# Layer normalisation from batch-norm statistics, a tile at a time, in a fused convolution, attention and expert kernel

## The reference

```python
x = x + _L0_conv_ref(_gn(x), L0_conv_weight)            # x: 8 x 64 x 56 x 56
t = _to_tokens(x)                                        # 8 images x 3136 tokens x 64 channels
t = t + _L1_attn_ref(_ln_t(t), Wq, bq, Wk, bk, Wv, bv)   # one head of 64
t = t + _L1_ffn_ref(_ln_t(t), gate_w, gate_b, w1, w2, w3)  # 16 experts, the best 2 of each token
x = _from_tokens(t, x)

def _ln_t(v, eps=1e-05):
    m = jnp.mean(v, axis=-1, keepdims=True)
    s = jnp.var(v, axis=-1, keepdims=True)
    return (v - m) / jnp.sqrt(s + eps)
```

## Time and profile before

| what | value |
|---|---|
| median of 3 runs | 2724.68 us (2722.92 to 2728.44) |
| the profiled execution | 2721.7 us, of which the span is 2720.0 us |
| TensorE busy | 2506.6 us (92%) |
| VectorE busy | 1832.1 us (67%), 5227 instructions |
| ACT busy | 1317.0 us (48%) |
| GpSimd busy | 1016.9 us (37%) |
| mean granted TensorE clock | 0.964 |

### The profile page before, as it was taken

How to read it: one execution, slowest core, us unless ns; L and a number is a source line. 1 busy time by engine, 2 the same in 40 slices (tenths; PEclk the granted TensorE clock), 3 DMA queues, 4 the chain that set the end, 5 groups by cost and what they waited for, 6 DMA issues and landing times.

```text
span 2720.0 us, 46270 instructions
## 1 busy us (share of the span) xinstructions
PE 2506.6 (92%) x13821; PEld 1604.3 (59%) x13821; DVE 1832.1 (67%) x5227; ACT 1317.0 (48%) x2986; POOL 1016.9 (37%) x1097
## 2 busy tenths in 40 slices
PE   5899999999999999999999999999999999997773
PEld 3455555566666666566666666566665656554662
DVE  5577677767676777677766777676867776674432
ACT  2344444455555555455545555455555555453542
POOL 2022005300343425342444324442344324465665
PEclk8899999999999999999999999999999999997866
DMA  2033101111112122121212122222121111122432
GB/s 75 26 90 77 45 22 48 49 34 39 53 49 66 52 54 59 55 58 49 62 52 62 48 57 64 58 53 53 54 55 52 43 49 51 54 55 62 121 94 53
DMA packets 226556, 152.95 MB, mean 56 GB/s; under 512 B 100240, under 2 KB 216720, under 8 KB 226320
## 3 DMA queue, kind: packets, MB, share of 16 engines
q1 hardware_dynamic: 190880, 98.26, 13.7%
q0 software_dynamic: 31456, 48.03, 6.8%
q10 hardware_dynamic: 3984, 3.70, 0.6%
HBM read 83.92 MB, written 65.27 MB: 55 GB/s over the span
## 4 chain that ended last, share of the span: by engine, by line
PE 62%; DVE 14%; issue 5%; DMA 2%; POOL 2%; ACT 1%; SPq 1%; POOLq 0%; DVEq 0%; ACTq 0%
PE ps_o L1480 16%; PE ps_s L1468 8%; PE ps_m L1440 7%; PE ps_s L1469 7%; DVE max_part L1118 4%; PE ps_x L1639 4%; PE ps_z L1653 3%; PE ps_z L1506 3%; PE ps_x L1646 2%; PE ps_z L1628 2%; DMA tc<-kept 1%; PE ps_y L1543 1%; PE ps_y L1559 1%; PE ps_s L1639 1%; POOL got L780 1%
## 5 line engine op out<-in xcount | busy, mean ns | idle before, releaser
L1118 DVE TENSOR_REDUCE max_part<-ps_m 128x1 f32<-128x448 f32 x1400 | 858.3, 621 | 517.1 <-PE ps_m L1440 497.1
L951 ACT ACTIVATE prob<-ps_s 128x448 f32<-128x448 f32 x1400 | 757.3, 543 | 526.6 <-PE ps_s L1469 502.8
L1480 PE MATMUL ps_o<-prob,v_s 128*64 128x448 f32 x2800 | 682.8, 561 | 0.0
L1468 PE MATMUL ps_s<-q_a,k_a 128*128 128x448 f32 x1400 | 592.7, 423 | 1.7 <-ACT q_a L943 0.7
L780 POOL DMA_INDIRECT got<-sorted_y,slot x448 | 427.3, 954 | 433.7 <-PE ps_s L1469 216.6
L759 POOL DMA_INDIRECT sorted_x<-xn,slot x448 | 428.8, 957 | 350.8 <-issue 154.7
L1440 PE MATMUL ps_m<-k_a,q_a 128*128 128x448 f32 (+3 forms) x1600 | 531.1, 359 | 27.1 <-DVE max_part L1118 21.2
L1469 PE MATMUL ps_s<-q_b,k_a 128*128 128x448 f32 x1400 | 511.4, 365 | 0.0
L1440 PEld LDWEIGHTS ps_m<-k_a,q_a 128*128 128x128 f32 (+1 forms) x1600 | 298.6, 188 | 92.2 <-DVE max_part L1118 61.2
L1468 PEld LDWEIGHTS ps_s<-q_a,k_a 128*128 128x128 f32 x1400 | 265.3, 189 | 142.4 <-ACT prob L951 107.3
L1480 PEld LDWEIGHTS ps_o<-prob,v_s 128*64 128x64 f32 x2800 | 153.2, 135 | 225.2 <-issue 161.7
(11 more groups left out here) (190 smaller groups left out, 3033.6 us busy)
## 6 DMA issues: line engine op xcount, KB each, us to landing
fx<-sorted_x SPq DMA_DIRECT2D x43, 384.0 KB
sorted_y<-fy SPq DMA_DIRECT2D x42, 320.0 KB, 2.9
xh<-in_x SPq DMA_DIRECT2D x96, 126.0 KB, 2.7
fx<-sorted_x SPq DMA_DIRECT2D x47, 256.0 KB
sorted_x<-fy POOLq DMA_DIRECT2D x28, 320.0 KB, 6.0
sorted_x<-xn,slot POOLq DMA_INDIRECT x448
got<-sorted_y,slot POOLq DMA_INDIRECT x448
x_now<-in_x SPq DMA_DIRECT2D x112, 56.0 KB, 2.3
```

Source lines behind the costliest of these rows:

```text
L951: a.activation(prob[(at.n * KEY_TILES + i) % PROBS][:], ps_s[(at.n * KEY_TILES + i) % 2][:, 0:CHUNK], ACT.Exp).then_inc(s["p_ready"], 1)
L1118: v.tensor_reduce(max_part[n % 2][0:here.stop - here.start, j, kb:kb + 1], ps_m[(passes_before(n) + m) % 2][0:here.stop - here.start, 0:CH ...
L1468: t.matmul(ps_s[t_of % 2][:, 0:CHUNK], k_a[p][:, keys], high, start=True, stop=False)
L1480: t.matmul(ps_o[side:side + CHANNELS, 0:CHUNK], v_s[u % 2][:, i, :], prob[(n * KEY_TILES + i) % PROBS][:], start=(i < 2), stop=(i >= KEY_T ...
```

## The change

Mean and variance now come from `bn_stats` (six numbers for a tile of 64 columns) and `bn_aggr` (mean and variance from these), for each of the four tiles of a chunk. The variance plus epsilon goes to GpSimd as before. The apply is a `tensor_scalar` for each tile, which takes the mean and the factor as two column operands and reads the tokens themselves, so the centred copy of norm 1 goes away. `centre` and `spread` become one event: norm 2 at step 6, norm 1 at step 10.

```diff
-         (4, "post", "attended"), (4, "post", "residual"), (6, "post", "norm2a"), (7, "post", "norm2b"), (8, "post", "apply2"),
-         (9, "stats", "stats"), (10, "post", "turned2"), (10, "pre", "norm1a"), (11, "post", "gate"), (11, "pre", "norm1b"),
+         (4, "post", "attended"), (4, "post", "residual"), (6, "post", "norm2"), (8, "post", "apply2"),
+         (9, "stats", "stats"), (10, "post", "turned2"), (11, "post", "gate"), (10, "pre", "norm1"),
...
-            def centre(link, source, ln_c, ln_s):
-
-                link(v.tensor_reduce(ln_s[:, 0, :], source, AX.X, ALU.add))
-                link(v.tensor_scalar(ln_s[:, 1, :], ln_s[:, 0, :], 1.0 / CHANNELS, None, ALU.mult))
-                link(v.tensor_tensor(ln_c[:], source, ln_s[:, 1, :].unsqueeze(2).to_broadcast([TILE, PER, CHANNELS]),
-                                     ALU.subtract))
-
-            def spread(link, ln_c, ln_s):
-
-                link(v.tensor_tensor(ln_q[:], ln_c[:], ln_c[:], ALU.mult))
-                link(v.tensor_reduce(ln_s[:, 1, :], ln_q[:], AX.X, ALU.add))
-                v.tensor_scalar(ln_s[:, 2, :], ln_s[:, 1, :], 1.0 / CHANNELS, LN_EPS, ALU.mult, ALU.add).then_inc(link.sem, 1)
+            def spread(link, source, which, ln_s):
+
+                for j in range(PER):
+                    last = v.bn_stats(ln_st[:, which, j, :], source[:, j, :])
+                link(last)
+                for j in range(PER):
+                    last = v.bn_aggr(ln_mv[:, which, j, :], ln_st[:, which, j, :])
+                link(last)
+                v.tensor_scalar(ln_s[:, 0, :], ln_mv[:, which, :, 1], LN_EPS, None, ALU.add).then_inc(link.sem, 1)
+
+            def normal(out, source, which, j, ln_s):
+
+                return v.tensor_scalar(out, source, ln_mv[:, which, j, 0:1], ln_s[:, 1, j:j + 1], ALU.subtract, ALU.mult)
...
-                    last = v.tensor_tensor(token, ln_c[:, here, KEYS], ln_s[:, 3, here].unsqueeze(2)
-                                           .to_broadcast([TILE, here.stop - here.start, CHANNELS - 1]), ALU.mult)
+                    for j in range(here.start, here.stop):
+                        last = normal(token[:, j - here.start, :], tok[:, n % TOKS * PER + j, KEYS], 0, j, ln_s)
...
-                link(v.tensor_tensor(ln2_c[:], ln2_c[:], ln2_s[:, 3, :].unsqueeze(2).to_broadcast([TILE, PER, CHANNELS]),
-                                     ALU.mult))
+                for j in range(PER):
+                    last = normal(ln2_c[:, j, :], t_now[:, j, :], 1, j, ln2_s)
+                link(last)
```

More of the change, by code:

```diff
@@ L421, in build @@
         tok = sb("tok", [TILE, TOKS * PER, CHANNELS])
-        ln_s = sb("ln_s", [TILE, 4, PER])
-        ln2_s = sb("ln2_s", [TILE, 4, PER])
-        ln_c = sb("ln_c", [TILE, PER, CHANNELS])
+        ln_s = sb("ln_s", [TILE, 2, PER])
+        ln2_s = sb("ln2_s", [TILE, 2, PER])
         ln2_c = sb("ln2_c", [TILE, PER, CHANNELS])
-        ln_q = sb("ln_q", [TILE, PER, CHANNELS])
+        ln_st = sb("ln_st", [TILE, 2, PER, 6])
+        ln_mv = sb("ln_mv", [TILE, 2, PER, 2])
         xn = sb("xn", [TILE, PER, 2, CHANNELS], f32r)
@@ L792, in norm1 @@
             def norm1(at):
-                wait_apart(pool, s["ln_link"], (at.index("pre") + 1) * 6)
-                g.tensor_tensor(ln_s[:, 3, :], ln_s[:, 2, :], minus_half[0:TILE, :], ALU.pow).then_inc(s["ln_rstd"], 1)
+                wait_apart(pool, s["ln_link"], (at.index("pre") + 1) * 3)
+                g.tensor_tensor(ln_s[:, 1, :], ln_s[:, 0, :], minus_half[0:TILE, :], ALU.pow).then_inc(s["ln_rstd"], 1)
             def norm2(at):
-                wait_apart(pool, s["ln2_link"], (at.index("post") + 1) * 6)
-                g.tensor_tensor(ln2_s[:, 3, :], ln2_s[:, 2, :], minus_half[0:TILE, :], ALU.pow).then_inc(s["r_rstd"], 1)
+                wait_apart(pool, s["ln2_link"], (at.index("post") + 1) * 3)
+                g.tensor_tensor(ln2_s[:, 1, :], ln2_s[:, 0, :], minus_half[0:TILE, :], ALU.pow).then_inc(s["r_rstd"], 1)
             def group_rstd(b):
@@ L1076, in conv, with norm1 @@
                     .then_inc(s["xconv_ready"], 1)
-            def norm1a(at):
+            def norm1(at):
                 n = at.index("pre")
                 dve.wait_ge(s["tok_ready"], n + 1)
-                centre(Link(dve, s["ln_link"], n * 6), tok[:, tokens_of(n), :], ln_c, ln_s)
-            def norm1b(at):
-                spread(Link(dve, s["ln_link"], at.index("pre") * 6 + 3), ln_c, ln_s)
+                spread(Link(dve, s["ln_link"], n * 3), tok[:, tokens_of(n), :], 0, ln_s)
             def apply1(at):
@@ L1148, in attended, with norm2 @@
                 last.then_inc(s["o_used"], 1)
-            def norm2a(at):
+            def norm2(at):
                 r = at.index("post")
                 dve.wait_ge(s["o_used"], r + 1)
-                centre(Link(dve, s["ln2_link"], r * 6), t_now[:], ln2_c, ln2_s)
-            def norm2b(at):
-                spread(Link(dve, s["ln2_link"], at.index("post") * 6 + 3), ln2_c, ln2_s)
+                spread(Link(dve, s["ln2_link"], r * 3), t_now, 1, ln2_s)
             def apply2(at):
@@ L1309, in combine @@
                 v.tensor_tensor(t_out[:, :, 0:CHANNELS], tc[k % 2][:], first[:], ALU.add).then_inc(s["c_ready"], 1)
-            events = {"normed": border, "convolved": conv, "norm1a": norm1a, "norm1b": norm1b,
-                      "apply1": apply1, "residual": attended, "norm2a": norm2a, "norm2b": norm2b, "apply2": apply2,
+            events = {"normed": border, "convolved": conv, "norm1": norm1,
+                      "apply1": apply1, "residual": attended, "norm2": norm2, "apply2": apply2,
                       "logits": logits, "picked": picked, "compared": compared,
@@ L1395, in _ @@
                 if place >= 1:
-                    norm1a(LEADS[place - 1])
-                    norm1b(LEADS[place - 1])
+                    norm1(LEADS[place - 1])
                 reduces(0, block[1:3])
```

## The result

The changed kernel took 2705.44 us in the median of four runs (2703.87 to 2710.95), the kernel before beside it 2723.8 us (2720.41 to 2728.44): ratio 0.9935, 95% interval 0.9914 to 0.9956. A second series of five runs on one chip gave 2704.4 us, ratio 0.9935 (0.9921 to 0.9948). It is faster by 0.65%, about 18 us, and 2703 was forecast. The time came out right by luck: two large terms behind it were wrong with opposite signs and nearly cancelled.

The account below looks back on a forecast made before the run. TensorE sets the main loop's time; VectorE counts only where TensorE waits for it. Terms 8.1, 3.7, 5.5, 1.5 and 2.9 give 21.7 us off 2721.7, so 2700.0; the median lies 3.0 higher: 2703, range 2691 to 2731.

Parts of the forecast that it names:

- The prices: VectorE's new instructions: normalisation 1.26 us (1.15 to 1.86), apply 0.89; together 2.15 us instead of 2.55.
- my upper bound: Apply on VectorE: four tensor_scalar take 1.15 us if the second column operand costs what the first adds.
- The rival that short instructions do not overlap: VectorE: each instruction waits for the one ahead to end; no gain, 2729 us. Chance 0.20 together with waits returning elsewhere.
- Early L1552: Transposes of xn2, 95 to 530 us: ten waits for q_b shortened by 0.81 us each, 8.1 us.
- Later L1552: Transposes of xn2, 530 to 2400 us: ten waits for q_b shortened by 0.37 us each, 3.7 us.
- the step on the second maximum: Later body at 1105.16 us: second maximum starts behind the product ending at 1107.83, so apply starts at 1108.37 instead of 1109.17.
- all 12 at L1524: 5.5: Transposes of xn, fed by apply1: all 12 waits vanish, the longest 0.7 us against 0.37 + 0.40; 5.5 us.
- Opening: Before 95 us: seven chunks in one chain through the normalisation, 0.4 us saved each, 2.9 us.
- The closing phase: End of the kernel, with TensorE's largest wait, 65.4 us for t_out behind gathers: unchanged.
- Late L1552: Transposes of xn2: three waits for xn shortened by about 0.5 us each, 1.5 us.
- The sum: Whole kernel: all terms together save 21.7 us, giving 2703 us; chance of this case 0.52.

Follow-up runs that it names:

- the split of the scale: Changed kernel with group normalisation's two last scale instructions, behind a VectorE wait for GpSimd, moved behind apply1: 2697.0 us, ratio 0.9909 to the kernel before.
- Norm 2 alone: New statistics event and apply for norm 2 only, norm 1 as in the kernel before: 2703.8 us, ratio 0.9922 to the kernel before.

## Why the prediction came out right

- **The prices held in sum.** Statistics were forecast at 0.21 us and took 0.21; aggregates 0.19 and 0.16; the apply 0.275 each and 0.31, for the second column costs another 0.06, which lay between the value that I took and my upper bound. The normalisation took 1.11 us (216.40 to 217.51; forecast 1.26), the apply 1.01 (219.11 to 220.12; forecast 0.89): 2.12 together, against 2.15. The two errors, 0.15 too dear and 0.12 too cheap, cancel in the sum only: the apply stands behind the power, on the path.
- **The rival that short instructions do not overlap fell.** Statistics start 0.126 us apart at 0.21 each, aggregates 0.066 at 0.15, the apply 0.222 at 0.31 (medians). The Trainium skill (VectorE: DVE Perf Modes, "The DRAIN you can't avoid") makes the next operation wait for an empty pipeline, and adds that one which is not held starts earlier. The rows, with 0.08 us of overlap at each of the three, agree with the addition and not with the rule.
- **Early L1552: mechanism right, size 0.66 us a body instead of 0.81.** The apply starts 2.71 us behind the normalisation's start, held by the second maximum, as forecast (2.69). It is then 0.12 us dearer than forecast. Ten bodies gave 6.5 us, 8.1 were forecast.
- **Later L1552: the step on the second maximum was wrong.** I took the product that ends at 1107.83 for the second maximum's and got 0.37 us. VectorE is one product behind there, so that each maximum reads the product ahead of the latest one: the pair of maxima ran through from 1101.39 without a wait, before the like product had started. The power sets the apply, at 2.51 us (my own sum for it was 2.56), and the wait fell from 1.23 to 0.33 us, by 0.90. The waits in this stretch fell by 6.9 us; 3.7 were forecast.
- **A term was missing: waits that the table of waits does not show.** Step 10 lasts 1.0 us where nothing holds it and lasted about 1.2 in 25 later bodies of before without a wait at L1552. TensorE in one of them, with VectorE's `q_b`:

```profile
977.54 0.62 DVE L1110 TENSOR_TENSOR q_b<-ps_y,q_a 128x448 fp32r<-128x448 f32 x1
...
978.01 0.36 PE L1440 MATMUL ps_m<-k_a,q_a 128*128 128x448 f32 x1
978.39 0.39 PEld L1552 LDWEIGHTS ps_y<-ident,xn 112*128 112x128 f32 x4 [0.38 <-issue]
978.42 0.57 PE L1552 MATMUL ps_y<-ident,xn 112*128 112x112 f32 x4
978.73 0.19 PEld L1468 LDWEIGHTS ps_s<-q_a,k_a 128*128 128x128 f32 x1
```

  and in the changed kernel:

```profile
972.89 0.62 DVE L1108 TENSOR_TENSOR q_b<-ps_y,q_a 128x448 fp32r<-128x448 f32 x1
...
973.69 0.36 PE L1435 MATMUL ps_m<-k_a,q_a 128*128 128x448 f32 x1
973.73 0.50 PEld L1547 LDWEIGHTS ps_y<-ident,xn 112*128 112x128 f32 x4
973.89 0.55 PE L1547 MATMUL ps_y<-ident,xn 112*128 112x112 f32 x4
974.18 0.19 PEld L1463 LDWEIGHTS ps_s<-q_a,k_a 128*128 128x128 f32 x1
```

  In the first the weight load starts 0.23 us behind the end of `q_b` (978.16), and the matmul has no idle time to show, for the product ahead ends at 978.37. Only the load's own gap shows it, put down to "issue". In the second `q_b` ends earlier (973.50), the load again starts 0.23 us behind that and lies under the product: from the product's start to the next step's load are 0.49 us instead of 0.72. Over the 33 later bodies without a wait at L1552 that is 5.7 us. With 6.6 us in the ten early bodies and 7.6 in the ten later ones that waited, these make nearly all of step 10's 20.3 us, where some 13 were forecast.
- **L1524: the step "all 12 at L1524: 5.5" failed.** I took it that `apply1` would come 0.40 us earlier for the normalisation's saving and that its dearer length was already paid. Its own start had not been looked at. Step 16 lost 5.7 us, at two places. In an image's last chunk `apply1` stands behind group normalisation's scale, which waits for GpSimd; the lead is lost there, and the dearer apply falls through to TensorE: 3.0 us in six bodies, as the split of the scale shows. In ten others, bodies 0 to 5 and 7 to 10, no scale stands there, and they lost 3.2 us (the remaining bodies gained 0.5). In most of these the lead is lost at the maximum ahead of `apply1`, which waits for TensorE's product, in one of them before:

```profile
192.09 0.62 DVE L1118 TENSOR_REDUCE max_part<-ps_m 128x1 f32<-128x448 f32 x1 [0.31 <-PE ps_m L1440]
192.63 0.41 DVE L1097 TENSOR_TENSOR v_s<-ln_c,ln_s 112x252 f32<-112x252 f32 x1
...
193.40 0.42 DVE L1105 TENSOR_TENSOR xn<-v_s,xn 112x252 fp32r<-112x252 f32 x1
...
194.01 0.54 PEld L1524 LDWEIGHTS ps_y<-ident,xn 112*128 112x128 f32 x4
```

  and in the changed kernel:

```profile
189.98 0.62 DVE L1116 TENSOR_REDUCE max_part<-ps_m 128x1 f32<-128x448 f32 x1 [0.31 <-PE ps_m L1435]
190.52 0.97 DVE L1029 TENSOR_SCALAR v_s<-tok,ln_mv,ln_s 112x63 f32<-112x63 f32 x4
...
191.86 0.42 DVE L1103 TENSOR_TENSOR xn<-v_s,xn 112x252 fp32r<-112x252 f32 x1
...
192.33 0.39 PEld L1519 LDWEIGHTS ps_y<-ident,xn 112*128 112x128 f32 x4 [0.44 <-DVE xn L1103]
```

  From the start of `apply1` to the end of `xn` are 1.19 us before and 1.76 here, and the weight load, which had no idle time ahead of it before, now waits for `xn`. Step 16 lasts 1.03 and 1.32 us in this body, and TensorE shows no wait at L1519 for it. Norm 2 alone shows that the whole 5.7 us are norm 1's.
- **Opening:** forecast 2.9 us. From the normalisation to the apply 2.40 us instead of 3.37, less 0.56 for the apply: 0.4 a chunk, as forecast (0.38 by the prediction's own terms, so that seven chunks are 2.7). But 1.7 arrived, and 0.6 to 3.3 in five other executions whose opening does the same. The closing phase, forecast unchanged, is some 2 us shorter here and 0.6 to 3.1 in the other profiled executions, which was not followed. **Late L1552:** 7.4 to 6.6 us, 0.8 of 1.5.
- **The sum.** 21.7 us were forecast, 18.2 lie between the two profiled executions. About 7 too little at step 10 and 11 too much at step 16 nearly cancel: the direction and the path through norm 2 were forecast and hold, but that 2703 lies so near to 2705 is luck.

The theory of the experiments was too narrow as well: cheaper statistics and the common place each hide most of the power without the other, and the change used up much of what both give in the dearer apply.

## What to carry to other kernels

Ask for the instruction that stands between the last input and the engine that waits, not for the engine's total. Shortening what lies ahead of another engine's round trip (here the power) pays until the trip is hidden, and what is then moved behind it (here the subtraction, fused into the apply) goes straight onto the path; one wide instruction in the shadow and one behind it beat four fused ones by 16 to 19 us here. A term that says "this wait vanishes" needs the waiting work's own start to be traced: the saving can be taken up by another wait in the same queue.

## What the runs showed of the hardware

- A column operand costs a 64-wide fp32 `tensor_scalar` 0.06 us each: 0.102, 0.162 and 0.222 us from start to start with none, one and two. Four with two columns (0.97 us) take over twice as long as one product over 256 with a broadcast operand (0.42). The Trainium skill (VectorE: DVE Perf Modes, "The perf-mode tier table") lets fp32 `tensor_scalar` from SBUF run at twice the rate of `tensor_tensor`, for 2048 elements; at 64 columns with column operands no row shows a gain by it.
- Four `bn_aggr` over six numbers take 0.38 us, 0.066 apart; four `bn_stats` over 64 columns 0.59 to 0.60, 0.126 apart. Mean and variance of 256 columns in four groups took 1.11 us with the small instruction behind them; the six instructions of before 2.09.
- TensorE lost 0.23 us in a body at step 10, and 0.29 in one at step 16, to a late weight load, without a wait at the matmul.
